# Relative index loaded in 16 KB and spread by TensorE, score bias of all four groups by ScalarE, and a new order on every engine

## What is computed

```python
x = x + conv(_ln_c(x), ...)           # window attention, 8x8 windows, 4 heads of 16
t = _to_tokens(x)
t = t + ffn(_ln_t(t), ...)            # 8 experts, the best 2 of each token
# conv:
qkv = xh @ w_qkv.T                     # split in windows of N = 64 tokens
bias = bias_table[rel_index.reshape(-1)].reshape(N, N, heads)
attn = softmax(einsum('whnd,whmd->whnm', q, k) * scale + bias)
out = einsum('whnm,whmd->whnd', attn, v) @ w_proj.T + b_proj
# ffn:
router_probs = softmax(x @ router_w + router_b)
top_p, top_i = top_k(router_probs, 2); top_p /= sum(top_p)
y = sum over the 2 picked experts of top_p * (x @ expert_w[e] + expert_b[e])
```

## Time and profile before

| | before |
|---|---|
| median of 3 runs | 1091.67 us (1088.63 to 1094.42) |
| the profiled execution's own time | 1087.85 us |
| its span, first to last instruction | 1086.1 us |
| PE busy | 1014.9 us (93%) |
| PEld busy | 576.0 us (53%) |
| DVE busy | 827.3 us (76%) |
| ACT busy | 797.9 us (73%) |
| POOL busy | 432.7 us (40%) |

### The profile page before, as it was taken

The page is one execution under the profiler, slowest core; times in us unless marked ns, Lnnn a source line. Parts: engine busy times, 40 slices in busy tenths (PEclk is TensorE's granted clock), DMA queues, the critical chain, the costliest instruction groups (busy, mean ns, idle before and its releaser), DMA issues.

```text
span 1086.1 us, 39091 instructions
## 1 busy us (share of the span) xinstructions
PE 1014.9 (93%) x16762; PEld 576.0 (53%) x16762; DVE 827.3 (76%) x1355; ACT 797.9 (73%) x1280; POOL 432.7 (40%) x509
## 2 busy tenths in 40 slices
PE   4898899999999999999999999999999999989867
PEld 3455555555555555556555555555555555555312
DVE  4456987877787787777787887777878877787775
ACT  1498888878787877878878888877888877667510
POOL 1002434334443443444434434444344346434550
PEclk9999999999999999999999999999999999999988
DMA  6003678987777898777787987777788876876885
GB/s 200 1 22 72 158 177 190 216 194 175 184 180 169 190 214 190 183 193 181 188 190 184 215 214 180 179 176 185 186 190 215 214 185 160 194 155 145 207 194 138
DMA packets 48872, 189.60 MB, mean 175 GB/s; under 512 B 10494, under 2 KB 10750, under 8 KB 32572
## 3 DMA queue, kind: packets, MB, share of 16 engines
q1 hardware_dynamic: 48700, 187.10, 72.5%
HBM read 151.15 MB, written 18.87 MB: 157 GB/s over the span
## 4 chain that ended last, share of the span: by engine, by line
PE 82%; DVE 6%; ACT 4%; issue 4%; POOL 1%; DMA 1%; SPq 0%; DVEq 0%; ACTq 0%; POOLq 0%
PE bank L711 19%; PE bank L590 12%; PE bank L607 11%; PE bank L624 7%; PE bank L564 5%; PE bank L534 5%; PE bank L631 5%; PE bank L574 4%; PE bank L643 3%; PE bank L652 2%; PE bank L662 2%; PE bank L511 2%; DVE gz L1870 2%; PE bank L525 1%; ACT lg L1279 1%
## 5 line engine op out<-in xcount | busy, mean ns | idle before, releaser
L711 PE MATMUL bank<-gz,wex 64*64 64x512 f32 x2048 | 254.0, 606 | 6.4 <-DVE ob L1919 4.8
L1848 DVE TENSOR_REDUCE mx<-bank 128x16 f32<-128x1024 f32 x128 | 156.1, 1220 | 112.2 <-PE bank L590 111.9
L1657 POOL TENSOR_TENSOR gz<-gz,tt 128x1024 f32<-128x1024 f32 x94 | 226.7, 2426 | 29.7 <-DMA gz<-gates_dram 29.7
L1870 DVE TENSOR_TENSOR gz<-gz,tt 128x1024 f32<-128x1024 f32 x156 | 202.2, 1314 | 1.1 <-DMA gz<-gates_dram 1.1
L1855 DVE TENSOR_TENSOR probs<-bank,mx 128x1024 f32<-128x1024 f32 x128 | 156.6, 1223 | 43.9 <-PE bank L607 40.8
L1618 POOL TENSOR_TENSOR tt<-prj,xs 128x512 f32<-128x512 f32 x64 | 82.7, 1316 | 250.8 <-ACT prj L1268 250.8
L607 PE MATMUL bank<-cst,probs 128*128 128x128 f32 x1024 | 166.6, 285 | 3.9 <-issue 2.1
L1251 ACT ACTIVATE pt<-bank 128x512 f32<-128x512 f32 x256 | 151.0, 590 | 24.7 <-PE bank L607 22.7
L607 PEld LDWEIGHTS bank<-cst,probs 128*128 128x128 f32 x1024 | 108.0, 140 | 100.1 <-issue 63.1
L590 PE MATMUL bank<-km,qs 32*64 32x128 f32 x4096 | 144.2, 276 | 4.1 <-issue 2.6
L590 PEld LDWEIGHTS bank<-km,qs 32*64 32x64 f32 x4096 | 112.4, 133 | 63.1 <-issue 62.4
(11 more groups left out here) (123 smaller groups left out, 1394.9 us busy)
## 6 DMA issues: line engine op xcount, KB each, us to landing
gz<-gates_dram SPq DMA_DIRECT2D x250, 512.0 KB, 7.9
xs<-in_x SPq DMA_DIRECT2D x32, 512.0 KB, 10.1
tx<-tt SPq DMA_DIRECT2D x128, 128.0 KB, 6.4
out<-ob SPq DMA_DIRECT2D x128, 128.0 KB, 6.0
gz<-in_rel SPq DMA_DIRECT2D x1, 2048.0 KB, 8.0
gates_dram<-gt_rs SPq DMA_DIRECT2D x32, 64.0 KB
cst<-in_consts SPq DMA_DIRECT2D x1, 359.0 KB, 2.9
tt<-in_weights SPq DMA_DIRECT2D x4, 64.0 KB, 3.8
```

Source lines behind the costliest of these rows:

```text
L711: last = mm(bank[64 * x:64 * x + 64, Y_BANK + a, :], wex[64 * a:64 * a + 64, e, :], gz[64 * a:64 * a + 64, s.pair(e)[1], e % 2, x * CH:(x ...
L1657: tt_(gz[:, k, e % 2, :], gz[:, k, e % 2, :], tt[s.buf(4)][:, :], op=ALU.mult).then_inc(z_pool, 1)
L1848: red(mx[g % 2][:, :], two_banks(S_BANK).rearrange("p (c k) -> p c k", k=N), axis=AX_X, op=ALU.max).then_inc(max_done, 1)
L1870: tt_(gz[:, k, e % 2, :], gz[:, k, e % 2, :], tt[s.buf(4)][:, :], op=ALU.mult).then_inc(z_dve, 1)
```

## The change

- `load_relative` reads the index once, as 8 rows of 512 (16 KB). VectorE turns it to bfloat16 (`relative_rows`), TensorE repeats each row over 128 partitions (`spread_relative`, 8 matmuls of 512 columns), ScalarE moves the result to SBUF in four pieces of 1024 (`move_relative`), and `one_hot` works on these pieces.
- `biases`, its constant and its split copy are gone. `seed_bias` fills the banks for every group of every strip, and every `scores` waits for it.
- The bias rows are summed in `Y_BANK` in place of `S_BANK`. The fourth strip's input is loaded ahead of the small expert loads.
- All five engines have a new order. On TensorE the loop is also cut at another place, and two expert multiplications have moved in among the groups.

```diff
@@ load_relative
-                sp.dma_start(rel_int, rel.rearrange("k q -> (k q)").partition_broadcast(P)).then_inc(rel_loaded, 16)
+                sp.dma_start(rel_int, rel.rearrange("k q -> (k q)").rearrange("(p n) -> p n", p=REL_ROWS)
+                             ).then_inc(rel_loaded, 16)
...
+            load(strips[3])
             load_expert_bias()
...
+            def spread_relative(j):
+
+                pe.wait_ge(rel_ready, 1)
+                if j == 3:
+                    pe.wait_ge(rel_moved, 1)
+                for n in range(2):
+                    k = 2 * j + n
+                    last = mm(bank[:, REL_BANKS[j] + n, :], row_pick[0:REL_ROWS, k:k + 1].broadcast_to([REL_ROWS, P]),
+                              rel_row, start=True, stop=True)
+                last.then_inc(rel_full, 1)
+
             def bias_rows():
 
-                pe.wait_ge(onehot_ready, 2)
+                pe.wait_ge(onehot_ready, 8)
+                pe.wait_ge(rel_moved, 2)
...
-            def biases(s, g):
-
-                if s.c == 0 and g == 0:
-                    pe.wait_ge(bias_ready, 1)
-                wait(pe, shift_done, s.count(GROUPS, g))
-                for hp in range(2):
-                    mm(bank[:, S_BANK + hp, :], tile_id[:, :],
-                       bias_hl[:, 2 * hp:2 * hp + 2, :].rearrange("p h k -> p (h k)").unsqueeze(1).broadcast_to(
-                           [P, 4, 2 * N]), start=True, stop=False, skip_group_check=True)
-
             def scores(s, g):
...
-                if g in SEEDED and s.c > 0:
-                    pe.wait_ge(seeded, s.count(len(SEEDED), SEEDED.index(g) + 1, lag=1))
+                pe.wait_ge(seeded[g % 2], s.count(2, g // 2 + 1))
...
+            def move_relative(j):
+
+                act.wait_ge(rel_full, j + 1)
+                af(rel_all[:, 1024 * j:1024 * j + 1024], two_banks(REL_BANKS[j]), ACT.Copy).then_inc(rel_moved, 1)
...
             def seed_bias(s, g):
 
-                act.wait_ge(shift_done, s.count(GROUPS, g))
+                if s.c == 0 and g == 0:
+                    act.wait_ge(bias_ready, 1)
+                wait(act, shift_done, s.count(GROUPS, g))
...
+            def one_hot(j):
+
+                dve.wait_ge(rel_moved, j + 1)
+                part = slice(1024 * j, 1024 * j + 1024)
                 for half in range(2):
-                    nc.vector.tensor_scalar(onehot[half].rearrange("p k q -> p (k q)"), rel_int,
+                    nc.vector.tensor_scalar(onehot[half].rearrange("p k q -> p (k q)")[:, part], rel_all[:, part],
                                             cv("row")[:, half:half + 1], None, ALU.is_equal).then_inc(onehot_ready, 1)
```

More of the change, by code:

```diff
@@ L742, in _ @@
             denominators(strips[0], 0)
+            transposes(strips[0], 3)
+            queries(strips[1])
+            scores(strips[0], 3)
             channel_sums(strips[2])
@@ L778, in _ @@
             transpose_logits(strips[0])
+            keys(strips[2])
             values(strips[1], 2)
@@ L809, in _ @@
             router(strips[1])
-            values(strips[2], 1)
+            transposes(strips[2], 4)
             transpose_logits(strips[1])
-            denominators(strips[2], 0)
-            transposes(strips[2], 4)
             keys(strips[3])
@@ L816, in _ @@
             experts(strips[0], 0)
+            values(strips[2], 3)
+            transposes(strips[2], 5)
             scores(strips[3], 0)
-            transposes(strips[2], 5)
+            denominators(strips[2], 1)
+            transposes(strips[2], 6)
             expert_bias_rows(strips[0])
-            values(strips[2], 3)
-            denominators(strips[2], 1)
+            transposes(strips[2], 7)
+            experts(strips[0], 1)
+            scores(strips[3], 1)
+            experts(strips[0], 2)
             spread_std(strips[4])
-            transposes(strips[2], 6)
-            biases(strips[3], 1)
-            scores(strips[3], 1)
-            transposes(strips[2], 7)
             values(strips[2], 4)
@@ L830, in _ @@
             transposes(strips[3], 0)
-            experts(strips[0], 1)
             transposes(strips[3], 1)
             transpose_gates(strips[1])
+            scores(strips[3], 2)
             values(strips[2], 6)
@@ L989, in _ @@
             experts(strips[-7], 1)
-            keys(strips[-3])
             experts(strips[-7], 2)
-            experts(strips[-7], 3)
-            experts(strips[-7], 4)
-            experts(strips[-7], 5)
             scores(strips[-3], 0)
-            transposes(strips[-4], 6)
-            spread_std(strips[-2])
             values(strips[-4], 4)
@@ L1025, in _ @@
             denominators(strips[-3], 0)
+            scores(strips[-3], 3)
+            queries(strips[-2])
+            experts(strips[-7], 7)
+            transposes(strips[-3], 2)
             channel_sums(strips[-1])
             router(strips[-4])
-            experts(strips[-6], 2)
+            transposes(strips[-3], 3)
             transpose_logits(strips[-4])
-            transposes(strips[-3], 4)
             values(strips[-3], 2)
@@ L1033, in _ @@
             denominators(strips[-3], 1)
-            transposes(strips[-3], 5)
-            experts(strips[-6], 3)
-            keys(strips[-2])
-            experts(strips[-6], 4)
-            experts(strips[-6], 5)
-            experts(strips[-6], 6)
+            transposes(strips[-3], 4)
+            experts(strips[-6], 0)
+            keys(strips[-2])
+            experts(strips[-6], 1)
+            experts(strips[-6], 2)
+            experts(strips[-6], 3)
+            experts(strips[-6], 4)
+            transposes(strips[-3], 5)
+            expert_bias_rows(strips[-6])
+            scores(strips[-2], 0)
+            transposes(strips[-3], 6)
             values(strips[-3], 4)
@@ L1087, in _ @@
             denominators(strips[-2], 2)
-            biases(strips[-1], 1)
             transposes(strips[-2], 7)
-            scores(strips[-1], 1)
             transpose_gates(strips[-3])
-            transposes(strips[-1], 0)
-            expert_bias_rows(strips[-5])
+            experts(strips[-5], 6)
             values(strips[-2], 6)
@@ L1143, in _ @@
             experts(strips[-3], 6)
-            expert_bias_rows(strips[-3])
+            router(strips[-1])
             experts(strips[-3], 7)
+            transpose_logits(strips[-1])
             experts(strips[-2], 0)
```

859 lines of the change are left out of this document (433 added, 426 removed).

## The result

The changed kernel took **1104.92 us** (median; 1102.18 to 1107.70) beside 1093.05 us for the kernel before on the same chip. The ratio is 1.0107, 95% interval 1.0074 to 1.0141: **slower by 1.1%**, where I forecast 1063 us.

What follows compares the result with a forecast made beforehand. TensorE was taken to bound each 30.81 us strip. Strips of 29.8 us save 27 us over 27 strips, the start 1 us: 1087.85 - 27 - 1 = 1060, plus 3.8 for the median, about 1063 us; forecast 1054 to 1072, range 1043 to 1085.

Steps and rivals of the forecast that it cites:

- DMA and order: Gate spreading and loads in new places on SP's queue: costed at nothing, gates being asked for most of a strip ahead.
- Group 3 to 0: Stretch between score starts of groups 3 and 0: two experts leave, other work comes; 14.9 us, as before.
- VectorE's lateness: Group 0's maxima on VectorE start up to 0.7 us late or not at all; 0.25 us a strip taken.
- Group 1 to 2: Stretch between score starts of groups 1 and 2: 5.0 us, with ScalarE's work from fill to fill ending last.
- the loop of scores and fill: Scores, maxima, shift, fill, scores through one pair of score banks: groups follow no faster than 4.77 us, three times a strip.
- Group 0 to 1 and 2 to 3: Stretches between score starts of these groups: 4.8 us for 0 to 1, 4.85 us for 2 to 3.
- What leaves TensorE: Each score bias costs TensorE 0.79 us; two leave each strip, 1.58 us, bounding the strip at 29.23 us.
- ScalarE as the bound: Rival, chance 0.10: ScalarE keeps three quarters of its idle time, a strip takes 31.4 us, total 1108 us, slower.
- The start: Before the first strip, the smaller index read and reordered bias work save 1 us.
- The rival of a start at full clock: Chance 0.12: early spreading matmuls raise TensorE's clock before the bias matmuls, 8 us less, 1055 us.
- The rule on TensorE's busy time: Skill's rule that matmul busy time is no fair measure; pointed to the no-change rival, about 1090 us, chance 0.09.

Runs made afterwards that it cites:

- x1: Changed kernel with expert 0's gate product moved on VectorE from ahead of the router's steps to the start of the next loop turn; 1092.79 us, ratio 1.0033.
- x9: Changed kernel with seven pairs of spread-gate buffers instead of six, and the gates' read for experts 0 and 1 ahead of the four token swaps; 1091.54 us, ratio 1.0001.
- x10: x1 plus gate transposes moved behind group 2's scores, and group 2's sums normalised ahead of `scale_x` on VectorE; 1089.72 us, ratio 1.0000.
- x8: Changed kernel's order, but TensorE again adds the score bias of groups 1 and 3, ScalarE filling only groups 0 and 2; 1110.04 us, ratio 1.0202.
- x12: x10 with expert 5 moved on TensorE from behind group 3's scores to ahead of the value rows; 1105.95 us, ratio 1.0116.

## Why the prediction was wrong

**DMA and order: the step that failed.** "I cost this at nothing, since the gates are asked for most of a strip ahead." That holds for the other pairs: the next one was asked for at 509.49 us and used at 535.28, 25.8 us later. The pair of expert 0 was asked for 12.84 us ahead before, with some 5.5 us to spare, and the new order took more, by a later read and by a longer transfer. The same step named what would follow, the row maxima behind the products, and that is what came. x1 and x9 open the loop by different means, from the two ends of the transfer, and both take it away: 12 and 13 us by the medians of the times, or 8 and 12 us by the ratios to the kernel before on the chip of each.

**Group 3 to 0: mis-sized by 0.23 us.** TensorE is dense there, as forecast, but I priced all experts at 1.0 us, which is one with another shape next to it. In a run of experts one takes 0.86 (two in 1.72 in the chain of x1). So what left was 2 x 0.86, what came 1.02 + 0.58 + 0.59: 14.90 + 0.47 = 15.37 against 15.38 measured. VectorE's lateness, for which I took 0.25, did not add to it.

**Group 1 to 2: mis-sized by 0.49 us, by the wrong engine.** I let ScalarE end last at 5.0. VectorE does: it has maxima, shift and `scale_x` in a row, and the transposed gates, which need `scale_x`'s bank, stand ahead of the scores. Scores, maxima, shift, `scale_x`, a pause and the transposed gates, 1.10 + 1.24 + 1.24 + 1.23 + 0.14 + 0.56, are 5.5 us, measured 5.49. x10 took the transposed gates out and the stretch fell to 4.83, about the loop of scores and fill.

**Group 0 to 1 and 2 to 3.** With the gates' loop open (x1) they are 4.84 and 4.77 against 4.8 and 4.85. The loop of 4.77 us through the one pair of score banks was right.

Together: an open loop leaves 30.48 us, 0.10 less than before, where I forecast 29.8; the transfer's loop adds 0.62, about half of the 1.30 us by which the strip is too long. So the cover of the gates explains why the kernel got slower, and the two mis-sized stretches why even x1 is no faster: of 1.58 us of TensorE's time that leave a strip, 0.47 is given back to moved work between groups 3 and 0, and about 1.0 to the stretches between the groups, where loops through VectorE and ScalarE end last. No single run isolates that second part.

**What leaves TensorE** was right in sign. x8 against x1 costs 0.84 us a strip, 0.64 of it between groups 0 and 1 and 0.37 between 2 and 3. I took 0.79 for each of the two biases. The two runs also differ in the place of expert 0's product, so no run measures a bias by itself.

**ScalarE as the bound** gave 1108 us, near the time measured by chance, and not for this reason. Two stretches (length, busy PE, PEld, DVE, ACT, POOL, granted clock, DMA share, GB/s), after and then x9:

```profile
500.00:531.50 31.50, 30.06 (x512) 16.99 (x511) 24.65 (x42) 26.65 (x43) 13.44 (x17) 1.00 0.82 188
```

```profile
500.00:530.80 30.80, 29.53 (x512) 16.80 (x510) 24.58 (x42) 26.62 (x42) 13.51 (x17) 1.00 0.82 190
```

ScalarE idles 4.85 us in after; with the same work x9 leaves it 4.18.

**The start** gained the 1 us forecast: the first scores start at 35.80 against 36.78 us. The rival of a start at full clock, ahead of the bias matmuls, fell:

```profile
18.19 7.00 PE L525 MATMUL bank<-tb,gz 128*64 128x12 bf16 x256
25.12 1.98 PE L559 MATMUL bank<-xr,wcen 64*64 64x512 f32 x8
...
35.80 1.10 PE L604 MATMUL bank<-km,qs 32*64 32x128 f32 x32 [0.41 <-issue]
```

7.00 us for 256 is the rate of 5.61 for 202, and the queries behind them still took 1.98. The granted clock reads 1.00 (2.4 GHz) over these rows, so it does not show the slow rate here either. The Trainium skill (TensorE: Matmul & The Clock Gate, Part 1) has sustained work release the clock; spreading the index and these small multiplications did not. What I had not foreseen is that the first scores took 1.10 us, where they took 1.98 before, so they ended 1.9 us sooner.

**The rule on TensorE's busy time** (the Trainium skill, Perfetto Trace Analysis, section Identifying the Most-Contended Engine) pointed to no gain, and with the loop open there was none (x1, x9, x10). The trace agrees with its verdict on busy time, which fell by 18 us while the kernel got slower; it was waits between engines, not ScalarE's occupancy, that took the gain.

## What to carry to other kernels

When an order changes, take each transfer by itself: when it is asked for, when its data are used, how long it takes, and the issues that now stand ahead of it on its queue; an average ("most of a strip ahead") hides the one with 5.5 us to spare, and a transfer's length may change with its place. A read may have several conditions, and opening one moves nothing if another ends as late, so list all of them before an edit. When work leaves the engine that is dense, write down for each stretch the next loop through the other engines, in their own order of instructions, and compare that with the dense time.

## Not expected of the hardware

TensorE now and then stood still with no wait that the profile shows, and in one case ran slowly behind it. In x12 it stood for 1.84 us up to 529.62 us; over the 3.8 us from 529.6 the granted clock was 0.55, close to the level of 1.2 GHz, and scores took 1.77 us in place of 1.10. Behind it, from 533.4, the clock was 1.00 again (columns as above):

```profile
529.60:533.40 3.80, 3.79 (x40) 2.96 (x40) 1.22 (x1) 1.40 (x2) 3.80 (x2) 0.55 0.01 4
```

In the kernel before it stood for 2.09 us up to 714.58 us, and the clock stayed at 1.00. What tells the two apart, and why TensorE stands, stays open.
